# First attention layer by chunk of queries, with the output projection, feed-forwards and linear layer of chunks 0 and 1 among its later cells

## The reference, cut to what matters

```
x = x + attn_a(layernorm(x))     # 16 heads of 16, softmax(mask * q k / sqrt(T)) v, then Wo
x = x + ffn(layernorm(x))        # silu(x Wg) * (x Wu), 1024 wide, then Wd
x = x + lin(layernorm(x))        # q * cumsum(k * v) over tokens, scaled, then Wo
x = x + ffn(layernorm(x))        # the same weights again
...                              # second attention (b), hyperbolic layer, third attention (c), hyperbolic layer
```

## Time and profile before

| | us |
|---|---|
| runs | 2732.45, 2735.32, 2740.95 |
| median | 2735.32 |
| profiled execution | 2741.86, of it span 2740.1 |

### The profile page before, as it was taken

One profiled execution on the slowest core, in us unless ns is written; L12 is line 12 of the kernel. 1 busy time (PEld: TensorE's weight loads), 2 busy tenths in 40 slices (PEclk: granted clock), 3 DMA queues, 4 the chain that ended last, 5 costly groups with the idle time before them and its releaser, 6 DMA issues. The chain is left out here.

```text
span 2740.1 us, 38483 instructions
## 1 busy us (share of the span) xinstructions
PE 2499.6 (91%) x13878; PEld 1264.1 (46%) x13878; DVE 1884.0 (69%) x4855; ACT 1231.1 (45%) x1494; POOL 149.0 (5%) x330
## 2 busy tenths in 40 slices
PE   6999999989999997999999999988779999999985
PEld 4544333335565554433333333334436556555644
DVE  5577888836345532889898988873847877776618
ACT  3234566761111112167676767665121345555540
POOL 2200111110000000000000000000000001010100
PEclk9756999999999998599999999999876999999998
DMA  6330312000000005210300300000173426262200
GB/s 201 90 40 2 47 17 32 1 20 1 1 1 0 12 1 173 31 16 1 47 1 1 47 1 2 1 1 16 39 205 94 99 80 112 70 111 70 55 1 31
DMA packets 68147, 121.51 MB, mean 44 GB/s; under 512 B 11890, under 2 KB 29554, under 8 KB 64370
## 3 DMA queue, kind: packets, MB, share of 16 engines
q1 hardware_dynamic: 67956, 119.06, 19.5%
HBM read 79.92 MB, written 38.27 MB: 43 GB/s over the span
## 5 line engine op out<-in xcount | busy, mean ns | idle before, releaser
L1093 ACT ACTIVATE PF<-PS 128x1024 f32<-128x1024 f32 (+3 forms) x1152 | 1053.6, 953 | 819.2 <-PE PS L932 491.5
L1309 DVE TENSOR_REDUCE MP<-PS 128x1 f32<-128x512 f32 x1408 | 877.8, 682 | 161.2 <-PE PS L871 156.0
L871 PE MATMUL PS<-KR,QR 48*128 48x512 f32 (+3 forms) x2304 | 784.4, 482 | 87.3 <-DVE MP L1309 34.8
L871 PEld LDWEIGHTS PS<-KR,QR 48*128 48x128 f32 x2304 | 357.5, 203 | 638.7 <-DVE MP L1309 325.8
L953 PE MATMUL PS<-PF,VO 128*32 128x512 f32 (+3 forms) x4608 | 606.6, 601 | 0.2
L932 PE MATMUL PS<-QR,KR 50*128 50x512 f32 (+3 forms) x2304 | 512.4, 431 | 25.9 <-DMA QR<-MRL 17.9
L1305 DVE CUSTOM_DVE_ANT_0 JUNK<-PS,WA 128x512 bf16<-128x512 f32 (+3 forms) x512 | 286.9, 605 | 102.1 <-PE PS L871 52.7
L932 PEld LDWEIGHTS PS<-QR,KR 50*128 50x128 f32 x2304 | 250.5, 197 | 212.6 <-ACT PF L1093 140.1
L741 PE MATMUL PS<-RQ,RK 64*128 64x512 f32 (+3 forms) x1920 | 274.5, 371 | 0.0
L735 PE MATMUL PS<-HT,WA 128*128 128x512 f32 x512 | 221.1, 592 | 0.0
L689 POOL TENSOR_SCALAR_AFFINE_SELECT PF<-PF 128x256 f32<-128x256 f32 x256 | 103.9, 409 | 2104.0 <-ACT PF L1093 2100.6
(11 more groups left out here) (139 smaller groups left out, 1434.1 us busy)
## 6 DMA issues: line engine op xcount, KB each, us to landing
WA<-rope_scores SPq DMA_DIRECT2D x66, 256.0 KB, 3.2
rope_scores<-WA SPq DMA_DIRECT2D x22, 256.0 KB, 2.7
QR<-parts_a_q SPq DMA_DIRECT2D x18, 256.0 KB, 6.1
KR<-parts_a_k SPq DMA_DIRECT2D x18, 256.0 KB, 9.5
QR<-parts_b_q SPq DMA_DIRECT2D x18, 256.0 KB, 11.3
KR<-parts_b_k SPq DMA_DIRECT2D x18, 256.0 KB, 14.6
QR<-parts_c_q SPq DMA_DIRECT2D x18, 256.0 KB, 6.5
KR<-parts_c_k SPq DMA_DIRECT2D x18, 256.0 KB, 9.4
```

Of the source, the lines that this page charges most:

```text
L871: mm(bank(slots[h][0], w), QR[rows, t0 + tb * P:t0 + (tb + 1) * P], KR[rows, t0 + s0:t0 + s0 + w], start=True, stop=True).then_inc(L.slot_ ...
L1093: sc.activation(PT[:, u % SETS, 2 * q:2 * q + 2, off:CH], src, ACT.Exp).then_inc(L.exp_done, 1)
L1309: ins = v.reduce_max(MP[:, i, c, y:y + 1], src, AX.X)
```

## The change

Layer "a" alone gets a new order and a new planner; "b" and "c" keep theirs. Its cells now go chunk by chunk, the four head groups of chunk 0 first. Since a cell's keys are then other heads than those of the cell before, keys are loaded anew for each cell, in batches of one chunk of keys for one cell (load_batch): 6 DMAs, and 6 more for the cell's queries in the first batch of each. A batch is issued when the unit that last reads its place has been scored; QR holds four cells' queries in its lower half. The upper half of QR is free for work tiles.

The output projection, both feed-forwards and the linear layer of chunks 0 and 1 (FILLED = 2) are cut into steps of two to four matmuls, and stand in L.steps from the first cell of chunk 1 on, evenly over what is left (`due`). They take banks from the same three (now least recently used first, since a down product holds one bank over four steps). The wave behind the layer is left with chunks 2 and 3; p1 does all four. The suffix products become eight steps of their own, between the first-pass steps of cell 1. VectorE does a norm in three steps, the residual additions, gate and up products and the scan; ScalarE copies and the tanh. Each bank gets a semaphore of its own in place of one count for all.

```diff
+FILLED = 2
+Q_CELLS = 4
+IN_RING = 4
+LOAD_TIME = 12.0
+def fill_steps(c):
+    def norm(r):
+        return [(0.0, 1.0, ("nm", c, r, j)) for j in range(3)] + [(0.5, (3.0, 0.0)[kk], ("nT", c, r, kk)) for kk in range(KD)]
+    def ffn(r):
+        out = []
+        for m in range(HID // P):
+            out += [(1.75, 1.5 if m == 0 else 0.0, ("fg", c, r, m)), (1.75, 0.0, ("fu", c, r, m))]
+        return out + [(1.75, 2.5 if (h, j) == (0, 0) else 0.0, ("fd", c, r, h, j)) for h in range(2) for j in range(4)]
+    out = [(0.5, (4.0, 0.0)[kk], ("oT", c, kk)) for kk in range(KD)] + [(1.75, (1.5, 0.0)[h], ("oP", c, h)) for h in range(2)]
+    out += norm(0) + ffn(0) + norm(1)
...
+    return out + norm(2) + ffn(1) + norm(3)
+        self.cells = [(g, c) for c in range(NC) for g in range(NG)] if by_chunk else [(g, c) for g in range(NG) for c in range(NC)]
+    def plan_by_chunk(self):
+        max_step = lambda n: (1.14 * self.jobs[n][5] / CH + 0.1, 0.66 * self.jobs[n][5] / CH + 0.1, ("max", n))
...
+            if cell == 1:
+                rests = [(0.0, 1.75, ("rest", n)) for n in range(NB // 2 - 1, -1, -1)]
...
+        fill_from = starts[NG]
...
+        for cost, step in twos:
+            if step[0] == "score" and step[1] in self.chunk_first and step[2] == 0:
+                cell = self.chunk_first.index(step[1])
+                while at <= max(at_step["mtr", cell], at_step["rest", 0]):
+                    give()
+                steps.append(("shift", cell))
+            room = 1.3
+            while at < len(ones) and given < target(run + cost / 2) and room > 0.1 and in_place():
+                room -= ones[at][0]
+                give()
...
+            for _ in range(2):
+                due = fill_total * (run - fill_from) / (whole - fill_from)
+                if fills and filled < due:
+                    weight, gap, fill = fills[0]
...
+                    if clock >= ready:
+                        fills.pop(0)
+                        steps.append(fill)
+                        filled += weight
+                        clock += weight
+                        last_fill = clock
+            steps.append(step)
...
+        self.steps = steps + [x for _, x in late] + [x for _, _, x in fills]
+            def load_batch(L, n):
+                cell, i, _ = L.batches[n]
+                g, c = L.cells[cell]
+                if n >= IN_RING:
+                    sp.wait_ge(L.batch_in[n % IN_RING], L.batch_count[n - IN_RING])
...
+                for m in range(3):
+                    for h in range(2):
+                        if i == 0:
...
+                            sp.dma_start(dst, src[h]).then_inc(L.batch_in[n % IN_RING], 16)
...
+                        sp.dma_start(dst, src[h]).then_inc(L.batch_in[n % IN_RING], 16)
+                        if L.by_chunk:
+                            if tb % BPC == 0 and p == 0:
+                                n = L.batch_no[L.cell_of(g, tb // BPC), i]
+                                pe.wait_ge(L.batch_in[n % IN_RING], L.batch_count[n])
+                if kind in ("fg", "fu"):
+                    W = WGT if kind == "fg" else WUT
+                    over_k(bank(slot), lambda kk: W[:, kk, m * P:(m + 1) * P], ht).then_inc(ready, 1)
...
+                if kind == "fg":
+                    dve.wait_ge(L.slot_ready[slot], uses)
+                    dve.wait_ge(under_tanh, n)
+                    v.scalar_tensor_tensor(out=TA_A[:], in0=TH_A[:, n % 2, :], scalar=1.0, in1=bank(slot),
+                                           op0=ALU.add, op1=ALU.mult).then_inc(free, 1)
...
-                   ("", wave("o0", "ffn", "lin", "ffn") + each("p1")), ("B", None),
+                   ("", wave("o0", "ffn", "lin", "ffn", first=FILLED) + each("p1")), ("B", None),
```

More of the change, by code:

```diff
@@ L101, in __init__ @@
         self.jobs = []
-        for g in range(NG):
-            for tb in range(NB):
+        for g, c in self.cells:
+            for tb in range(BPC * c, BPC * (c + 1)):
                 end = (tb + 1) * P if causal else T
@@ L131, in __init__, with cell_of, q_col, k_col @@
         self.chain = s("chain")
+    def cell_of(self, g, c):
+        return self.cells.index((g, c))
+    def q_col(self, g, c, p):
+        if self.by_chunk:
+            return (self.cell_of(g, c) % Q_CELLS * NP + p) * CH
+        return (g % 2 * NP + p) * T + c * CH
+    def k_col(self, g, c, p):
+        if self.by_chunk:
+            cell = self.cell_of(g, c)
+            return (cell % 2 * NP + p) * T + (2 * CH * (cell // 2 % 2) if c < 2 else 0)
+        return (g % 2 * NP + p) * T
+    def plan_batches(self):
+        self.batches, reader = [], {}
+        after = -1
+        for cell, (g, c) in enumerate(self.cells):
+            k0 = self.k_col(g, c, 0)
+            for i in range(c + 1):
+                after = max(after, reader.get((k0 // CH) + i, -1))
+                if i == 0 and cell >= Q_CELLS:
+                    after = max(after, self.chunk_last[cell - Q_CELLS])
+                self.batches.append((cell, i, after))
+            for i in range(c + 1):
+                reader[(k0 // CH) + i] = self.chunk_first[cell] + BPC * (i + 1) - 1
+        self.batch_no = {(cell, i): n for n, (cell, i, _) in enumerate(self.batches)}
+        self.batch_count, done = [], [0] * IN_RING
+        for n, (cell, i, _) in enumerate(self.batches):
+            done[n % IN_RING] += 16 * 6 * (2 if i == 0 else 1)
+            self.batch_count.append(done[n % IN_RING])
+    def place(self):
+        uses, order, held = [0] * SLOTS, list(range(SLOTS)), None
+        self.slot_at, self.taken = {}, []
+        for step in self.steps:
+            slots = []
+            if step[0] == "fd" and step[4] > 0:
+                if step[4] == 3:
+                    held = None
+            else:
+                for _ in range(TAKES.get(step[0], 0)):
+                    slot = next(x for x in order if x != held)
+                    order.remove(slot)
+                    order.append(slot)
+                    uses[slot] += 1
+                    slots.append((slot, uses[slot]))
+            if step[0] == "fd" and step[4] == 0:
+                held = slots[0][0]
+            assert not slots or step not in self.slot_at
+            if slots:
+                self.slot_at[step] = slots
+            self.taken.append([(x, n) for x, n in enumerate(uses) if n])
     def diagonal(self, u):
@@ L386, in build @@
         start.append(("rest", 0))
-        PROGRAM = [("in", start), ("A", None), ("", wave("o0", "ffn", "lin", "ffn") + each("p1")), ("B", None),
+        PROGRAM = [("in", start), ("A", None), ("", wave("o0", "ffn", "lin", "ffn", first=FILLED) + each("p1")), ("B", None),
                    ("", wave("o1", "hyp", "p2")), ("C", None), ("", wave("o2", "hypout"))]
@@ L673, in attention_steps @@
                         cell = step[1]
-                        g, c = divmod(cell, NC)
+                        g, c = L.cells[cell]
+                        x = cell % 2
+                        for half in range(2):
+                            slot, uses = L.slot_at["rest", 2 * c + half][0]
+                            pool.wait_ge(L.slot_free[slot], uses)
                         pool.wait_ge(L.shift_exp, cell + 1)
@@ L1152, in residual @@
+            c_under = Count()
             def residual(c):
```

492 lines of the change are left out of this document (376 added, 116 removed).

## The result

The changed kernel takes 2888.76 us (median of 4 runs, 2885.71 to 2898.06) where the kernel before took 2738.14 beside it: a ratio of 1.055 (95% interval 1.052 to 1.059). Forecast were 2653, and a range up to 2735. The change is slower by 5.5%.

What follows compares the result with a forecast made beforehand. The wave was taken as TensorE-bound, layer a's middle as bound by VectorE with three PSUM banks. Layer a +122 and the wave -204 gave net -82, so 2653 us from a median of 2735.3; range 2575 to 2735.

Steps and rivals of the forecast that it cites:

- I cost the streaming at nothing past chunk 0.: Layer a's key and query loads: hidden by cell length, at no cost; late batches bounded between 0 and 70 us.
- I take the 85% that the fullest engine reaches: Layer a's filled part: 485 us of TensorE array time at 85% use gives 570 us, bounds 497 and 634.
- 200 us of free array time: Layer a before the change: 320 us of array time in 524, so some 200 us free for moved work.
- the filled part: Layer a's cells 4 to 15: 485 us of array time, 443 of VectorE, forecast to take 570 us.
- Full clock soon after 157: Layer a once fills start: whole-array products bring the granted clock to full soon after 157 us.
- Start of layer a: Layer a's opening: first score at about 112 us, chunk 0 ending near 157, 74 us from the start.
- The wave: Work left behind layer a, chunks 2 and 3: 225 us in place of 428.7, saving 204.
- B: Rival: hardly any fill work is hidden in layer a; filled part 634, net -18, 2717 us; chance 0.13.
- C: Rival: the three PSUM banks become layer a's bound; filled part 697, net +45, 2780 us; chance 0.1.
- D: Rival: clock stays low beside the fills for 140 us more, costing 50 us, total 2703; chance 0.09.
- E: Rival: the plan does not place its fills, which run behind the last cell; no change, 2735 us; chance 0.03.

Runs made afterwards that it cites:

- order_only: Changed kernel with FILLED = 0: chunk order, streamed keys and spread suffix products kept, nothing of the wave moved; 2887.9 us, 1.057 of the kernel before.
- nokeys_f0: Changed kernel with FILLED = 0 and no keys loaded past the first two cells, so an even first-pass plan; 2770.3 us, 1.011 of the kernel before.
- nokeys: Changed kernel with all fills (FILLED = 2) but no keys loaded past the first two cells; 2832.3 us, 1.033 of the kernel before.
- nk_banks5_f0: nokeys_f0 with five banks for first pass and transposes and one score pair, in place of three and two; 2896.8 us, 1.058 of the kernel before.
- nk_skel: nokeys with filled gate, up, down products streaming a quarter of their columns, and tanh, gate and up evictions on 32 of 512; 2764.4 us, 1.005.
- nk_banks5: nokeys with five banks for first pass and fills and one score pair, in place of three and two; 2862.6 us, 1.046 of the kernel before.
- nk_fdone: nokeys with the four steps of each down group in a row, not spread over two or more units; 2818.4 us, 1.026 of the kernel before.
- before_warm: Kernel before, with an overwritten whole-array product ahead of each score pair of layer a's first 24 units; 2759.3 us, 1.007 of the kernel before.

## Why the prediction was wrong

*"I cost the streaming at nothing past chunk 0."* This is the first step that failed. I priced its DMA issues and the case that a batch lands late, bounded by 70 us, and TensorE indeed never waited for one. But I had the planner's text before me, with in_place() and LOAD_TIME, and did not ask what else gives way when a step must wait in the plan: it does not run later beside other work, it bunches. The runs show 118 us without fills (order_only against nokeys_f0), 112 of them by the uneven plan alone, and 56 with fills (the changed kernel against nokeys). So in the changed kernel it is the smaller part of the 236 us between 2888.8 and 2653: with no streaming cost at all nokeys still stands at 2832, 179 above the forecast.

*"I take the 85% that the fullest engine reaches", so 485/0.85 = 570.* The second, and in the changed kernel the larger. The 85% was VectorE's busy share in the stretch from 260 to 560; of TensorE's array I had counted 75% there myself (485/0.75 is 647), and the whole layer gives less. Counting matmuls at their full-clock spacing as in the earlier trace rows, and dividing by the granted clock, gives the array time; against the time of layer a from the first score on:

```
                array, full clock   at granted clock   time   share
before                 278                331           484     68%
nokeys_f0              278                356           510     70%
order_only             278                420           624     67%
nk_banks5_f0           278                383           639     60%
nokeys                 487                561           769     73%
nk_skel                368                488           707     69%
nk_banks5              487                553           820     67%
after                  487                580           824     70%
```

With two score pairs the array is used 67 to 73% of the time, whatever is put in (nk_fdone, the best, 74%); with one pair 60%, and 67% with fills. So most of the "200 us of free array time" was no room for a fill. The same 209 us of fills add 180 us to layer a where the share was 60% (nk_banks5, 667.3 to 847.7), 201 at 67% (order_only) and 260 at 70% (nokeys_f0). That the unused part is short latencies inside each unit's chain, which each added product brings with it anew, is my reading and not shown. For the filled part (201 to 957): 461 of array time by count (I had 485), 533 at the granted clock of 0.87, 533/0.705 = 756. So of the miss of 182 us the clock makes some 85 (461 to 533, divided by 0.85), the share 129, and my count gave 28 back. Where the fills paid for themselves, in order_only's empty thirds and beside one score pair, the kernel without them had holes that had cost more before. The table also shows the clock's part in the uneven plan: of the 114 us from nokeys_f0 to order_only 64 are array time at the granted clock.

What stayed open: how the fills' 260 us in the even plan divide. The work of the thinned products is 67 (nk_skel, net of a falling clock), the tanh hop some 20 and the held down banks some 20, both within the noise of their intervals, the placing nothing measurable; the rest, over half, was not taken apart.

*Clock.* "Full clock soon after 157" was wrong as a steady state: 0.84 in layer a, with full clock in places only. That whole-array products raise it was right (1.00 in before_warm, 0.98 in the wave). Narrow ones alone do not always hold it: in the dense half of a cell TensorE is 10.00 of 10 us busy at 0.50. The Trainium skill, page "TensorE: Matmul & The Clock Gate", section "The HAM clock gate", would have sustained activity release it; these rows again do not agree. But narrow products can run at full clock: the even plan's cell has them at 1.00 from 535 to 562. What decides between the two is not shown.

*Start of layer a.* First score at 129 (forecast 112), of it 12 from the first stage; chunk 0's end at 201 (forecast 157). Chunk 0 ran at a clock of 0.59 from 129 to 197 with the cells' first pass in front of each score, and I had added up VectorE's and SyncE's parts as if they lay side by side.

*The wave.* 225 us forecast, 222 measured. Right, and the projections behind it unchanged, as said.

*The rivals.* B, "hardly anything is hidden", had the right outcome for the fills (201 added for 209) with a price too low for the part, as it started from 425 without fills: by nokeys_f0 that part takes 438, by order_only some 550. C had the sign and the waits in view, but the one bank hold that was tested is some 20 us, within the noise (nk_fdone); TensorE's waits for reductions rose to 41 us, far from the 127 by which it lengthened the part. D's low clock came in part, spread over the layer: 0.87 in the filled part. E did not: all but four steps were placed. No rival had the uneven plan.

## What to carry to other kernels

Before work is moved under a phase, compare the phase's time with its array time at the granted clock; if that share stays near the same when the content changes (here 67 to 74%), the rest is not free room, and moved work can take its full price and more (209 us of array time cost 201 and 260). Don't carry one engine's busy share over to another's array time. Where a plan must hold steps back for data, count how the held steps bunch afterwards: two engines that were busy side by side then take turns, the clock can fall with it, and neither the busy share of the fullest engine nor any DMA wait shows it; the windows inside one loop body do.

## What was not expected of the hardware

Taking away 119 of 487 us of array time in layer a made untouched products 16% longer (508 to 588 ns) through the granted clock (0.84 to 0.68 in layer a). And the clock rose to 1.00 over 95 us by whole-array products of no use, at a net cost of 17 us.
